# Three chunks of the last down product moved into the next turn, down products over three banks, and rows for outputs copied later

## The chip, the cores and the metric

One core of a Trainium2 chip runs the whole kernel. The metric is the device time of one execution in microseconds (us), lower is better. The engines are TensorE (PE for its matmuls, PEld for its weight loads), VectorE (DVE), ScalarE (ACT), GpSimd (POOL) and SyncE (SP), which issues the DMAs. Matmul results land in eight PSUM banks of 128 x 512 floats.

## The reference, cut to what matters

The kernel computes one decoder block on four sequences of 512 rows of 512 channels, in float32:

```
x = x + attention(layernorm(x))                    # 16 heads of 128
x = x + gamma * xattn(layernorm(x), ctx, ctx)      # 8 heads; a head is 64 rows of the sequence
h = layernorm(x)
x = x + (silu(h @ w1q.T) * (h @ w3q.T)) @ w2q.T    # 1365 hidden units, weights quantised to -s, 0, s
```

(The third layer norm is drawn in for the reader: the reference applies it to the argument of the feed-forward part.) The change touches the last two lines, computed for one sequence after another.

## The kernel before, in words

Stage A (to about 722 us) is the attention of all sequences. Stage B is the rest, and the change lies in it. Every product is done in two or three passes over a high and a low part of its operand, to keep float32's accuracy: so every tile has a part `...h` and a part `...l`, ScalarE writes the first, VectorE or GpSimd the second.

Stage B is a list of turns, `turns` (L411): (b, f) = (1, 0), (2, 1), (3, 2), (None, 3). A turn does the cross attention of sequence b beside the feed-forward part of sequence f, the one before it. All engines have their order written out by hand, in functions `pe_turn`, `act_turn`, `dve_turn`, `pool_turn` and `sp_rows`, and meet at semaphores. An engine does its instructions strictly in that order.

The first part of a turn has 32 steps n = 4h + q: head h of 8, query tile q of 4. In a step PE does one score tile (`pe_sx`, two matmuls of 512 columns into bank 0 or 1), the four transposes of a probability tile of the head before (`pe_pt`), in steps q = 1 and 3 half of a result (`pe_ret`, eight matmuls of 256 columns into bank 4), and one or no piece of the up product (`pe_up`). There are 22 pieces, for 11 chunks of hidden units (the last has 85) times the two weights w1 and w3; a piece is eight matmuls into bank 5 (w1) or bank 6 (w3). Piece 0, in step 1, comes in two halves of 256 columns, since the transposed rows `x3h` and `x3l` that it reads are only just made. ScalarE takes tanh, VectorE multiplies up (`dve_up`) and the gated hidden units lie in `gth` and `gtl`.

A score tile's bank is free again once VectorE has its row maximum (`dve_max`) and ScalarE its exponential (`act_exp`); with two banks, tile n + 2 waits for tile n. VectorE adds a head's result to the rows `x2` (`dve_ret`, two instructions, done for head h - 2 in steps with q = 2 from h = 2 on), and this also frees bank 4 (`r_free`) for the next head's `pe_ret`.

The end of a turn: `pe_down` for the four row tiles t = 0 to 3 of sequence f, each 11 chunks of two matmuls (22 of 512 columns) into `y_bank[t % 2]`, which is bank 7 or bank 5. Beside it VectorE makes the layer norm of sequence b (`dve_x3`, `dve_x3n`). PE then transposes tiles 0 and 1 of it (`pe_x3`), does the down product of t = 3, and transposes tiles 2 and 3; ScalarE writes `x3h` (`act_x3`), VectorE `x3l` (`dve_x3l`), which the next turn's piece 0 waits for. `dve_y` adds a down product to the rows `x2res`, and SP stores them to the output.

The rows `x2` are wanted twice: as the residual `x2res` of sequence f = b, and their place is filled with the next sequence's rows. In the first steps of the next turn GpSimd copies them tile by tile (`pool_keep`, L947, after all four output stores have landed), in steps 0 to 3. SP waits for the fourth copy and then loads the new 1 MB `x2` (L469), which `dve_ret` of head 0 waits for in step 10 (L787). In SP's order this load stands between the loads of head 2 and of head 3; each head has four loads of 128 KB (`sp_head`). They and this load go through one hardware queue.

Of the kernel before, what the change touches and what calls it, by code (L numbers as in the profile page):

```python
# [25 lines left out]
P = 128  # L26
B, T, C = 4, 512, 512
CK = C // P
TJ = T // P
# [6 lines left out]
XH, XD = 8, 64  # L36
SCALE_X = float(XD) ** -0.5
HID = int(2 * C * 4 / 3)
HC = -(-HID // P)
# [10 lines left out]
TANH_LAG, GATE_LAG = 1, 1  # L50
WARM = 34
RING_A = 4
WT = WS // 2
TERNARY = 3 * HID * C // WP // WT
SLOTS = 3 * CK + CK - 1
# [125 lines left out]
def decoder_block(nc, x, ctx, ctx_cols, wk, wq, wo, wvt, bk, bq, bv_col, bo, gamma, w1t, w3t, w2t, out):  # L181
# [7 lines left out]
    with stack:  # L189
# [129 lines left out]
        gth, gtl = put("gth", 136 * KB, [P, HC, T], F32R), put("gtl", 158 * KB, [P, HC, T], F32R)  # L319
        w2 = put("w2", 180 * KB, [P, HC, C], F32R)  # L320
        mem.close()
        u_bank, y_bank = bank[5:7], [bank[7], bank[5]]
        main = Mem(x1d=x1d, kd=kd, vd=vd, qst=qst, kh=kh, kl=kl, vts=vts, pe_x=pe_x, pxh=pxh, pxl=pxl, x2=x2,
                   s=bank[0:2], t=bank[2:4], r=bank[4], ring=2)

# [53 lines left out]
        def kept(f):  # L379
            return 16 + f * TJ  # L380
# [73 lines left out]
        def sp_rows(sp, b, f):  # L454

            if b is not None:
                sp.wait_ge(s[f"x1_out{b}"], 16)
                sp.wait_ge(s[f"st_out{b}"], 16)
                sp_stats(sp, b)
                sp_head(sp, main, b, 0)  # L460
                sp_head(sp, main, b, 1)
            if f is not None:
                for t in range(TJ):
                    sp.wait_ge(s["y"], 1 + f * TJ + (t + 1))
                    sp.dma_start(rows(out, f)[t * P:(t + 1) * P, :], x2res[:, t, :]).then_inc(s["y_out"], 16)
            if b is not None:
                sp_head(sp, main, b, 2)
                sp.wait_ge(s["x2_kept"], kept(b - 1))
                sp.dma_start(main.x2[:], rows(x1_dram, b).rearrange("(t p) c -> p t c", p=P)).then_inc(s["x2_in"], 16)  # L469
                for h in range(3, XH):  # L470
                    sp_head(sp, main, b, h)

        def sp_x2_back(sp):
# [95 lines left out]
        def pe_up(pe, f, piece):  # L569
            i, w = piece // 2, piece % 2  # L570
            m = chunk_rows(i)
            if piece == 0:
                pe.wait_ge(s["w_in"], 32)
                pe.wait_ge(s["out_free"], PASSES * GROUPS * PB * HG)
                pe.wait_ge(s["y"], 1 + f * TJ)
            pe.wait_ge(s[f"u{w}_free"], 1 + f * HC + i)

            for cols in (slice(0, T // 2), slice(T // 2, T)) if piece == 0 else (slice(0, T),):
                if piece == 0:
                    pe.wait_ge(s["t_free"], t_x3(f, cols.stop // P))  # L580
                for c in range(CK):
                    lhs = w13[:, w, c, i * P:i * P + m]
                    pe.matmul(u_bank[w][0:m, cols], lhs, x3h[:, c, cols], start=c == 0, stop=False)  # L583
                    mm = pe.matmul(u_bank[w][0:m, cols], lhs, x3l[:, c, cols], start=False, stop=c == CK - 1)  # L584
            mm.then_inc(s[f"u{w}_ready"], 1)

        def pe_down(pe, f, t, chunks=range(HC)):
            if 0 in chunks and t == 0:
                pe.wait_ge(s["w2_in"], 32)
            if 0 in chunks and t >= 2:  # L590
                pe.wait_ge(s["y"], 1 + f * TJ + (t - 1))
            if 0 in chunks and t == 1:
                pe.wait_ge(s["u0_free"], 1 + f * HC + HC)
            for i in chunks:
                k = chunk_rows(i)
                if t == 0:
                    pe.wait_ge(s["gl2"], 1 + f * HC + i + 1)
                pe.matmul(y_bank[t % 2][:], gth[0:k, i, t * P:(t + 1) * P], w2[0:k, i, :], start=i == 0, stop=False)  # L598
                mm = pe.matmul(y_bank[t % 2][:], gtl[0:k, i, t * P:(t + 1) * P], w2[0:k, i, :], start=False, stop=i == HC - 1)  # L599
            if HC - 1 in chunks:  # L600
                mm.then_inc(s["y_ready"], 1)

# [8 lines left out]
        def pe_turn(pe, b, f, nxt):  # L611
            for h in range(XH):
                for q in range(4):
                    if b is not None:
                        pe_sx(pe, main, b, h, q)
                        if h:
                            pe_pt(pe, main, b, h - 1, q)
                        if q == 1 and h >= 2:
                            pe_ret(pe, main, b, h - 2, 1)
                        if q == 3 and h >= 1:  # L620
                            pe_ret(pe, main, b, h - 1, 0)
                    if f is not None:
                        for piece in pieces(4 * h + q):
                            pe_up(pe, f, piece)
            if b is not None:
                pe_pt(pe, main, b, XH - 1, 0)
                pe_ret(pe, main, b, XH - 2, 1)
                pe_pt(pe, main, b, XH - 1, 1)
            if f is not None:
                pe_down(pe, f, 0, range(0, HC // 2))  # L630
            if b is not None:
                pe_pt(pe, main, b, XH - 1, 2)
            if f is not None:
                pe_down(pe, f, 0, range(HC // 2, HC))
            if b is not None:
                pe_pt(pe, main, b, XH - 1, 3)
                pe_ret(pe, main, b, XH - 1, 0)
            if f is not None:
                pe_down(pe, f, 1, range(0, 3))
            if b is not None:  # L640
                pe_ret(pe, main, b, XH - 1, 1)
            if f is not None:
                pe_down(pe, f, 1, range(3, HC))
                pe_down(pe, f, 2)
            if b is not None:
                pe_x3(pe, b, 0)
                pe_x3(pe, b, 1)
            if f is not None:
                pe_down(pe, f, TJ - 1)
            if b is not None:  # L650
                for t in range(2, TJ):
                    pe_x3(pe, b, t)
# [159 lines left out]
        def dve_y(dve, f, t):  # L812
            dve.wait_ge(s["y_ready"], f * TJ + (t + 1))
            if t == 0:
                dve.wait_ge(s["x2_kept"], kept(f))
            dve.scalar_tensor_tensor(x2res[:, t, :], y_bank[t % 2][:], wmean[:, 2:3], x2res[:, t, :],
                                     ALU.mult, ALU.add).then_inc(s["y"], 1)

        def dve_back(dve, link, k):
# [43 lines left out]
        def dve_turn(dve, b, f, nxt, between=None):  # L863
            for n in range(S_TILES):
                h, q = n // 4, n % 4
                if b is not None:
                    if q == 2 and h >= 2:
                        dve_ret(dve, main, b, h - 2)
                    dve_max(dve, main, b, h, q)
                if f is not None:  # L870
                    for piece in pieces(n - TANH_LAG):
                        dve_up(dve, f, piece)
                if b is not None:
                    if h:
                        dve_px(dve, main, b, h - 1, q)
                    if n:
                        dve_rinv(dve, main, b, (n - 1) // 4, (n - 1) % 4)
                    if prep_step(h) == n:
                        dve_q(dve, main, b, h + 1)
                    if q == 3 and h >= 4 and h % 2 == 0:  # L880
                        dve_moments(dve, main, b, (h - 4) // 2)
                    if between:
                        between(n)
# [25 lines left out]
            if b is not None:  # L909
                dve_x3l(dve, b, 0)  # L910
                dve_x3l(dve, b, 1)
            if f is not None:
                dve_y(dve, f, TJ - 1)
            if b is not None:
                for t in range(2, TJ):
# [43 lines left out]
        def pool_turn(pool, b, f, nxt):  # L959
            for n in range(S_TILES):  # L960
                h, q = n // 4, n % 4
                if b is not None:
                    if n:
                        pool_prob(pool, main, b, (n - 1) // 4, (n - 1) % 4)
                    if prep_step(h) == n - 1:
                        pool_prep(pool, main, b, h + 1)
                    if n - 1 in map(values_step, range(0, XH, 2)):
                        pool_vt(pool, main, b, (n - 1) // 8 * 2)
                if f is not None:
                    if f and n < TJ:  # L970
                        pool_keep(pool, f, n)
                    for piece in pieces(n - GATE_LAG):
                        pool_up(pool, f, piece)
            if b is not None:
                pool_prob(pool, main, b, XH - 1, 3)
            if f is not None:
                for n in range(S_TILES, S_TILES + GATE_LAG):
                    for piece in pieces(n - GATE_LAG):
                        pool_up(pool, f, piece)
            if nxt is not None:  # L980
                pool_prep(pool, main, nxt, 0)
                pool_prep(pool, main, nxt, 1)
# [1305 lines left out]
```

## Time and profile before

| | |
|---|---|
| time of three runs | 1113.26, 1113.51, 1113.57 us; median 1113.51 us |
| the profiled execution's own time | 1112.65 us |
| its span, first to last instruction | 1110.5 us |
| granted TensorE clock, mean | 1.00 of 2.4 GHz |
| PE busy | 1104.1 us, 99% of the span |
| DVE, ACT, POOL busy | 734.5, 550.0, 480.8 us |
| DMA | 122.20 MB, mean 110 GB/s |

Times within the profile are in us from the span's start. A matmul of 512 columns has a duration of 0.39 us in the rows, but the next one starts 0.23 us after it: they are pipelined, so what PE needs for a row of matmuls is read from start to start. For 256 columns the step is 0.12 us, for a transpose of 128 columns 0.10 us. A row may stand for several instructions (x2, x4, x8), and then has their duration together. In the square brackets stands how long the engine had been idle, and what released it.

### The profile page before, as it was taken

What the parts mean: (1) busy time and instruction counts of PE and PEld (TensorE: products, weight loads), DVE (VectorE), ACT (ScalarE), POOL (GpSimd) and SP (SyncE); (2) the same over time, 40 slices, a digit from 0 to 9 for tenths busy, and PEclk for the clock granted to TensorE, in tenths of its full rate; (3) what the DMA queues carried; (4) which work ended last, traced back from release to release, by engine and by line L of the source; (5) the groups of instructions that cost most, each with busy time, mean ns of one, the idle gap of its engine ahead of it and who ended that gap; (6) DMA issues with size and microseconds to landing.
All of it is one profiled execution on the core that took longest, in us unless ns stands there. A gap on an engine that the chain in (4) does not pass through costs nothing.

```text
span 1110.5 us, 15911 instructions
## 1 busy us (share of the span) xinstructions
PE 1104.1 (99%) x5840; PEld 939.0 (85%) x5840; DVE 734.5 (66%) x1347; ACT 550.0 (50%) x1149; POOL 480.8 (43%) x430
## 2 busy tenths in 40 slices
PE   9999999999999999999999999999999999999998
PEld 8888888888888888888888888888888888888886
DVE  7555547787877688866424344689967876887531
ACT  4556673325143376667605233177627763775130
POOL 1322345341324375665344040157628762875130
PEclk9999999999999999999999999999999999999999
DMA  7566553544533724212630221462213211410101
GB/s 247 164 190 189 184 178 124 177 126 152 182 109 94 229 96 143 86 39 86 253 114 2 75 86 39 139 205 66 54 50 100 76 49 58 114 48 2 38 1 38
DMA packets 54664, 122.20 MB, mean 110 GB/s; under 512 B 10058, under 2 KB 10058, under 8 KB 52539
## 3 DMA queue, kind: packets, MB, share of 16 engines
q1 hardware_dynamic: 54586, 121.18, 33.8%
q8 instruction: 47, 0.77, 0.3%
q14 instruction: 31, 0.25, 0.1%
HBM read 103.32 MB, written 17.84 MB: 109 GB/s over the span
## 4 chain that ended last, share of the span: by engine, by line
PE 97%; DVE 1%; ACT 1%; DMA 0%; issue 0%; POOL 0%; SPq 0%; POOLq 0%
PE bank L176 20%; PE bank L177 20%; PE bank L178 20%; PE bank L583 7%; PE bank L584 7%; PE bank L541 5%; PE bank L599 4%; PE bank L598 4%; PE bank L565 3%; PE bank L566 3%; PE bank L551 3%; PE bank L552 3%; PE bank L608 0%; DVE x3l L860 0%; PE bank L1278 0%; DMA xnf<-in_x 0%
## 5 line engine op out<-in xcount | busy, mean ns | idle before, releaser
L583 PE MATMUL bank<-x3h,w 128*128 128x512 f32 (+2 forms) x368 | 143.5, 393 | 0.4 <-DVE x3l L860 0.3
L584 PE MATMUL bank<-x3l,w 128*128 128x512 f32 (+2 forms) x368 | 140.6, 385 | 0.0
L1471 ACT ACTIVATE yh<-bank 128x512 fp32r<-128x512 f32 x64 | 38.1, 599 | 205.2 <-PE bank L178 205.2
L2152 POOL TENSOR_TENSOR wbl<-raw_b,wbh 128x512 fp32r<-128x512 f32 x64 | 85.7, 1358 | 58.6 <-ACT wbh L1534 58.2
L940 POOL TENSOR_SCALAR pe_x<-pe_x,xri,gam 128x512 f32<-128x512 f32 x96 | 75.5, 787 | 77.8 <-DVE xri L779 75.3
L775 DVE TENSOR_REDUCE xmx<-bank 128x1 f32<-128x512 f32 x128 | 87.7, 687 | 31.8 <-PE bank L552 30.5
L176 PE MATMUL bank<-wah,gh 128*128 128x512 f32 x256 | 102.6, 401 | 0.0
L176 PE MATMUL bank<-yh,rh 128*128 128x512 f32 x256 | 100.4, 392 | 0.1
L176 PE MATMUL bank<-wah,ph 128*128 128x512 f32 x256 | 100.1, 391 | 0.0
L177 PE MATMUL bank<-wal,gh 128*128 128x512 f32 x256 | 100.1, 391 | 0.0
L178 PE MATMUL bank<-wah,gl 128*128 128x512 f32 x256 | 100.0, 391 | 0.0
L178 PE MATMUL bank<-yh,rl 128*128 128x512 f32 x256 | 99.8, 390 | 0.0
L177 PE MATMUL bank<-wal,ph 128*128 128x512 f32 x256 | 99.7, 390 | 0.0
L178 PE MATMUL bank<-wah,pl 128*128 128x512 f32 x256 | 99.7, 389 | 0.0
L177 PE MATMUL bank<-yl,rh 128*128 128x512 f32 x256 | 99.7, 389 | 0.0
L2147 POOL TENSOR_TENSOR wal<-raw_a,wah 128x512 fp32r<-128x512 f32 x44 | 61.9, 1433 | 77.2 <-ACT wah L1513 77.2
L1803 DVE TENSOR_TENSOR yl<-bank,yh 128x512 fp32r<-128x512 f32 x64 | 44.0, 690 | 74.6 <-ACT yh L1471 74.6
L1983 DVE SCALAR_TENSOR_TENSOR xacc<-bank,rinv,xacc 128x512 f32<-128x512 f32 x64 | 47.9, 749 | 68.2 <-PE bank L178 66.7
L697 ACT ACTIVATE pe_x<-bank,xmx 128x512 f32<-128x512 f32 x96 | 66.0, 688 | 31.7 <-DVE xmx L775 31.3
L583 PEld LDWEIGHTS bank<-x3h,w 128*128 128x128 f32 (+1 forms) x368 | 68.2, 185 | 15.0 <-DVE x3l L860 0.7
L584 PEld LDWEIGHTS bank<-x3l,w 128*128 128x128 f32 (+1 forms) x368 | 68.2, 185 | 12.8
L1803 DVE TENSOR_TENSOR ml<-bank,mh 128x512 fp32r<-128x512 f32 x64 | 43.6, 686 | 53.0 <-ACT mh L1471 53.0
(181 smaller groups left out, 3016.6 us busy)
## 6 DMA issues: line engine op xcount, KB each, us to landing
raw_a<-in_wk SPq DMA_DIRECT2D x8, 1024.0 KB, 5.2
raw_b<-in_wq SPq DMA_DIRECT2D x8, 1024.0 KB, 6.7
raw_a<-in_wo SPq DMA_DIRECT2D x8, 1024.0 KB, 5.3
raw_b<-in_wvt SPq DMA_DIRECT2D x8, 1024.0 KB, 4.9
ternary_scratch<-wraw SPq DMA_DIRECT2D x24, 341.2 KB, 3.0
x1d<-x_scratch SPq DMA_DIRECT2D x48, 128.0 KB, 3.2
kd<-in_ctx SPq DMA_DIRECT2D x48, 128.0 KB, 3.2
w<-ternary_scratch SPq DMA_DIRECT2D x2, 2730.0 KB, 11.3
```

Source lines behind the costliest of these rows:

```text
L176: pe.matmul(out, wh, xh, start=start, stop=False, skip_group_check=shared)
L177: pe.matmul(out, wh, xl, start=False, stop=False, skip_group_check=shared)
L178: return pe.matmul(out, wl, xh, start=False, stop=stop, skip_group_check=shared)
L541: mm = pe.transpose(tb[:, c * P:(c + 1) * P], m.pe_x[:, q, c * P:(c + 1) * P], ident[:])
L583: pe.matmul(u_bank[w][0:m, cols], lhs, x3h[:, c, cols], start=c == 0, stop=False)
L584: mm = pe.matmul(u_bank[w][0:m, cols], lhs, x3l[:, c, cols], start=False, stop=c == CK - 1)
L697: act.activation(m.pe_x[:, q, :], m.s[q % 2][:], ACT.Exp, bias=xmx[:, q:q + 1], accum_out=xrs[:, q:q + 1]).then_inc(s["s_free"], 1)
L775: dve.reduce_max(xmx[:, q:q + 1], m.s[q % 2][:], axis=AX, negate=True).then_inc(s["xmx"], 1)
L940: pool.tensor_scalar(m.pe_x[:, q, :], m.pe_x[:, q, :], xri[:, q:q + 1], gam[:], ALU.mult, ALU.mult).then_inc(s["xpn"], 1)
L1803: dve.tensor_tensor(dst, a_bank(u)[:, cols], high.bitcast(F32), ALU.subtract).then_inc(s["a_free"], 1)
L2147: pool.tensor_tensor(wal[:, c, :], raw_a[:, c, :], wah[:, c, :].bitcast(F32), ALU.subtract).then_inc(s["wal_pool"], 1)
L2152: pool.tensor_tensor(wbl[:, c, :], raw_b[:, c, :], wbh[:, c, :].bitcast(F32), ALU.subtract).then_inc(s["wbl"], 1)
```

## The change

- Of the last down product (t = 3) of a sequence, PE does chunks 0 to 7 where it stood, and the last three (`DOWN_LATE`) in the next turn, after the score tile of step 1 and before piece 0. `dve_y` of this tile moves to step 1 of the next turn, after the row maximum of that step. The last turn has no next one and keeps its order.
- The four down products get banks 7, 5, 6 and 7. The waits follow: t = 2 waits for the last w3 piece to be read and no longer for the output of t = 0; t = 3 waits for the output of t = 0 only; pieces 0 and 1 wait for the outputs of t = 1 and t = 2 of the turn before, not for all four; t = 0 waits for the output of t = 3 of the turn before.
- GpSimd's copies `pool_keep` move from steps 0 to 3 to steps 3 to 6.
- SP's loads of head 3 move ahead of the wait for the copies and of the `x2` load behind it.

```diff
--- before.py
+++ after.py
@@ -50,6 +50,8 @@
 TANH_LAG, GATE_LAG = 1, 1
 WARM = 34
 RING_A = 4
+
+DOWN_LATE = 3
 WT = WS // 2
 TERNARY = 3 * HID * C // WP // WT
 SLOTS = 3 * CK + CK - 1
@@ -319,7 +321,7 @@
         gth, gtl = put("gth", 136 * KB, [P, HC, T], F32R), put("gtl", 158 * KB, [P, HC, T], F32R)
         w2 = put("w2", 180 * KB, [P, HC, C], F32R)
         mem.close()
-        u_bank, y_bank = bank[5:7], [bank[7], bank[5]]
+        u_bank, y_bank = bank[5:7], [bank[7], bank[5], bank[6], bank[7]]
         main = Mem(x1d=x1d, kd=kd, vd=vd, qst=qst, kh=kh, kl=kl, vts=vts, pe_x=pe_x, pxh=pxh, pxl=pxl, x2=x2,
                    s=bank[0:2], t=bank[2:4], r=bank[4], ring=2)
 
@@ -465,9 +467,10 @@
                     sp.dma_start(rows(out, f)[t * P:(t + 1) * P, :], x2res[:, t, :]).then_inc(s["y_out"], 16)
             if b is not None:
                 sp_head(sp, main, b, 2)
+                sp_head(sp, main, b, 3)
                 sp.wait_ge(s["x2_kept"], kept(b - 1))
                 sp.dma_start(main.x2[:], rows(x1_dram, b).rearrange("(t p) c -> p t c", p=P)).then_inc(s["x2_in"], 16)
-                for h in range(3, XH):
+                for h in range(4, XH):
                     sp_head(sp, main, b, h)
 
         def sp_x2_back(sp):
@@ -572,7 +575,9 @@
             if piece == 0:
                 pe.wait_ge(s["w_in"], 32)
                 pe.wait_ge(s["out_free"], PASSES * GROUPS * PB * HG)
-                pe.wait_ge(s["y"], 1 + f * TJ)
+            if piece < 2:
+
+                pe.wait_ge(s["y"], 1 + (f * TJ - 2 + piece if f else 0))
             pe.wait_ge(s[f"u{w}_free"], 1 + f * HC + i)
 
             for cols in (slice(0, T // 2), slice(T // 2, T)) if piece == 0 else (slice(0, T),):
@@ -587,16 +592,20 @@
         def pe_down(pe, f, t, chunks=range(HC)):
             if 0 in chunks and t == 0:
                 pe.wait_ge(s["w2_in"], 32)
-            if 0 in chunks and t >= 2:
-                pe.wait_ge(s["y"], 1 + f * TJ + (t - 1))
             if 0 in chunks and t == 1:
                 pe.wait_ge(s["u0_free"], 1 + f * HC + HC)
+            if 0 in chunks and t == 2:
+                pe.wait_ge(s["u1_free"], 1 + f * HC + HC)
+            if 0 in chunks and t == 0 and f:
+                pe.wait_ge(s["y"], 1 + f * TJ)
+            if 0 in chunks and t == TJ - 1:
+                pe.wait_ge(s["y"], 1 + f * TJ + 1)
             for i in chunks:
                 k = chunk_rows(i)
                 if t == 0:
                     pe.wait_ge(s["gl2"], 1 + f * HC + i + 1)
-                pe.matmul(y_bank[t % 2][:], gth[0:k, i, t * P:(t + 1) * P], w2[0:k, i, :], start=i == 0, stop=False)
-                mm = pe.matmul(y_bank[t % 2][:], gtl[0:k, i, t * P:(t + 1) * P], w2[0:k, i, :], start=False, stop=i == HC - 1)
+                pe.matmul(y_bank[t][:], gth[0:k, i, t * P:(t + 1) * P], w2[0:k, i, :], start=i == 0, stop=False)
+                mm = pe.matmul(y_bank[t][:], gtl[0:k, i, t * P:(t + 1) * P], w2[0:k, i, :], start=False, stop=i == HC - 1)
             if HC - 1 in chunks:
                 mm.then_inc(s["y_ready"], 1)
 
@@ -619,6 +628,8 @@
                             pe_ret(pe, main, b, h - 2, 1)
                         if q == 3 and h >= 1:
                             pe_ret(pe, main, b, h - 1, 0)
+                    if f and h == 0 and q == 1:
+                        pe_down(pe, f - 1, TJ - 1, range(HC - DOWN_LATE, HC))
                     if f is not None:
                         for piece in pieces(4 * h + q):
                             pe_up(pe, f, piece)
@@ -646,7 +657,7 @@
                 pe_x3(pe, b, 0)
                 pe_x3(pe, b, 1)
             if f is not None:
-                pe_down(pe, f, TJ - 1)
+                pe_down(pe, f, TJ - 1, range(HC if b is None else HC - DOWN_LATE))
             if b is not None:
                 for t in range(2, TJ):
                     pe_x3(pe, b, t)
@@ -813,7 +824,7 @@
             dve.wait_ge(s["y_ready"], f * TJ + (t + 1))
             if t == 0:
                 dve.wait_ge(s["x2_kept"], kept(f))
-            dve.scalar_tensor_tensor(x2res[:, t, :], y_bank[t % 2][:], wmean[:, 2:3], x2res[:, t, :],
+            dve.scalar_tensor_tensor(x2res[:, t, :], y_bank[t][:], wmean[:, 2:3], x2res[:, t, :],
                                      ALU.mult, ALU.add).then_inc(s["y"], 1)
 
         def dve_back(dve, link, k):
@@ -867,6 +878,8 @@
                     if q == 2 and h >= 2:
                         dve_ret(dve, main, b, h - 2)
                     dve_max(dve, main, b, h, q)
+                if f and n == 1:
+                    dve_y(dve, f - 1, TJ - 1)
                 if f is not None:
                     for piece in pieces(n - TANH_LAG):
                         dve_up(dve, f, piece)
@@ -909,7 +922,7 @@
             if b is not None:
                 dve_x3l(dve, b, 0)
                 dve_x3l(dve, b, 1)
-            if f is not None:
+            if f is not None and b is None:
                 dve_y(dve, f, TJ - 1)
             if b is not None:
                 for t in range(2, TJ):
@@ -967,8 +980,8 @@
                     if n - 1 in map(values_step, range(0, XH, 2)):
                         pool_vt(pool, main, b, (n - 1) // 8 * 2)
                 if f is not None:
-                    if f and n < TJ:
-                        pool_keep(pool, f, n)
+                    if f and 3 <= n < 3 + TJ:
+                        pool_keep(pool, f, n - 3)
                     for piece in pieces(n - GATE_LAG):
                         pool_up(pool, f, piece)
             if b is not None:
```

## Rows read from the trace of the kernel before

**Rows 1.** The page: shares of the chain that ended last, by engine.

```profile
PE 97%; DVE 1%; ACT 1%; DMA 0%; issue 0%; POOL 0%; SPq 0%; POOLq 0%
```

**Rows 2.** Stretches: PE, PEld, DVE, ACT, POOL busy; clock, DMA share, GB/s.

```profile
827.00:835.00 8.00, 7.86 (x47) 6.74 (x46) 4.09 (x7) 3.65 (x9) 1.94 (x3) 1.00 0.31 100
835.00:934.00 99.00, 99.00 (x562) 83.95 (x561) 80.73 (x167) 61.83 (x134) 64.89 (x64) 1.00 0.22 67
...
1042.00:1050.00 8.00, 7.62 (x44) 6.36 (x44) 2.73 (x4) 1.78 (x3) 2.21 (x4) 1.00 0.09 35
```

**Rows 3.** Timeline, PE alone, first to second sequence: start, duration, engine, line.

```profile
827.87 0.39 PE L598 MATMUL bank<-w,gth 128*128 128x512 f32 x1
...
829.25 1.04 PE L608 MATMUL bank<-ident,pe_x 128*128 128x128 f32 x8
830.04 0.48 PE L551 MATMUL bank<-kh,qst 128*128 128x512 f32 x1
...
832.85 0.28 PE L584 MATMUL bank<-x3l,w 128*128 128x256 f32 x1
833.27 0.50 PE L551 MATMUL bank<-kh,qst 128*128 128x512 f32 x1
```

**Rows 4.** Timeline, DVE and ACT, the same place.

```profile
831.72 1.28 DVE L775 TENSOR_REDUCE xmx<-bank 128x1 f32<-128x512 f32 x2
...
832.44 0.69 ACT L697 ACTIVATE pe_x<-bank,xmx 128x512 f32<-128x512 f32 x1 [1.46 <-DVE xmx L775]
```

**Rows 5.** Timeline, all engines, where the last turn begins.

```profile
1044.34 1.04 PE L608 MATMUL bank<-ident,pe_x 128*128 128x128 f32 x8
1044.54 0.75 DVE L816 SCALAR_TENSOR_TENSOR x2res<-bank,wmean,x2res 128x512 f32<-128x512 f32 x1 [3.55 <-PE bank L599]
...
1045.50 0.36 PE L583 MATMUL bank<-x3h,w 128*128 128x256 f32 x1
...
1045.61 1.29 DVE L860 TENSOR_TENSOR x3l<-bank,x3h 128x512 fp32r<-128x512 f32 x2 [0.32 <-ACT x3h L719]
...
1046.40 0.28 PE L584 MATMUL bank<-x3l,w 128*128 128x256 f32 x1
...
1046.95 0.39 PE L583 MATMUL bank<-x3h,w 128*128 128x256 f32 x1 [0.26 <-DVE x3l L860]
```

**Rows 6.** Timeline, POOL, early in the second sequence's turn.

```profile
839.27 0.61 POOL L950 COPY x2res<-x 128x512 f32<-128x512 f32 x1
...
842.23 0.77 POOL L940 TENSOR_SCALAR pe_x<-pe_x,xri,gam 128x512 f32<-128x512 f32 x1 [0.16 <-DVE xri L779]
...
844.40 1.30 POOL L934 TENSOR_TENSOR qst<-x1d,qst 64x512 fp32r<-64x512 f32 x1
845.94 0.77 POOL L940 TENSOR_SCALAR pe_x<-pe_x,xri,gam 128x512 f32<-128x512 f32 x1 [0.24 <-DVE xri L779]
```

**Rows 7.** Timeline, SP's DMA queue, the same turn.

```profile
832.45 1.06 SPq L436 DMA_DIRECT2D kd<-in_ctx  x1
...
839.91 0.38 SPq L469 DMA_DIRECT2D x<-x_scratch  x1
```

**Rows 8.** Timeline, ACT, the keys of head 2.

```profile
839.41 0.63 ACT L667 ACTIVATE kh<-kd 128x512 fp32r<-128x512 f32 x1
```

**Rows 9.** Landing of loads: all of x2, then kd from 825 to 850 us.

```profile
DMA to landing us min/median/max: 5.9/6.3/7.0
...
DMA to landing us min/median/max: 3.2/3.7/6.1
```

**Rows 10.** The page: a 1 MB load elsewhere; count, size, median us to landing.

```profile
raw_a<-in_wk SPq DMA_DIRECT2D x8, 1024.0 KB, 5.2
```

**Rows 11.** Timeline, DVE: the result of head 0 added to x2.

```profile
851.66 0.66 DVE L788 TENSOR_TENSOR x<-x,bank 64x512 f32<-64x512 f32 x1
852.36 0.69 DVE L790 TENSOR_TENSOR x<-x,bank 64x512 f32<-64x512 f32 x1
```

**Rows 12.** Timeline, PE: the next use of bank 4.

```profile
854.51 0.36 PE L565 MATMUL bank<-pxh,vts 128*128 128x256 f32 x1
```

## The prediction, made before the change was run

> **What bounds the kernel now.** The first view to read is the chain of what ended last: 97% of it is PE [rows 1]. The table of stretches says where PE is not busy in stage B: in the 99 us of a turn's middle it is busy for all 99.00, and in the 8 us around a change of sequence it loses 0.14 us by that count, around the start of the last turn 0.38 us [rows 2]. These counts are too kind, since a matmul's modelled end hides part of a gap, so the third view is the timeline of those places, read from start to start. The change takes no matmul away. It can only gain what PE loses at the three changes of sequence with a down product behind them (near 830, 938 and 1045 us), and it can lose whatever the moved copies and loads set off.
>
> **PE's work, moved.** Six matmuls (three chunks, two passes) leave the end of a turn. Before, the last six took from 827.87 to 829.25, which is 1.38 us [rows 3]. They come back after the second score tile, at the same step of 0.23 us. Net 0. What moves is everything between: the transposes of tiles 2 and 3 and both score tiles come 1.38 us earlier, piece 0 comes at the same time.
>
> **Gain at the second and third sequence.** The last half-width matmul of piece 0 starts at 832.85; the next could follow 0.12 us later, at 832.97, but the third score tile starts at 833.27. That is 0.30 us, and it has a duration of 0.50 instead of 0.39 us, since the pipeline was empty: 0.40 us in all [rows 3]. It waits for the first score bank: two row maxima from 831.72, the exponential from 832.44 to 833.13, having waited for the maximum [rows 4]. All of that hangs on the transposes and so comes 1.38 us earlier, the bank is free near 831.75, and PE asks at 832.97. The cover is 1.2 us. The displaced `dve_y` does not stand in this chain: it comes after both maxima, which end at 831.72 + 1.28 - 1.38 = 831.62, with its product ready at about 831.05 + 0.2; it runs to 832.37. Behind it the first reciprocal is late by about 0.4 us against what it could be, and GpSimd's scaling with it, but that is still 0.9 us earlier than before. The same pattern stands at 940.4 to 940.8. Gain 2 x 0.40 = 0.80 us.
>
> **Gain at the last turn.** No score tiles stand there. The eight transposes from 1044.34 take 0.79 us (829.25 to 830.04 in rows 3), but piece 0 begins at 1045.50 and not at 1045.13: it waits for the output of t = 3 to be added (1044.54 + 0.75 = 1045.29), 0.37 us. After its first half, at 1046.40 + 0.12, it waits for `x3l`, of which two tiles run from 1045.61 to 1046.90, until 1046.95: 0.43 us, and 0.11 us more duration [rows 5]. With the change piece 0 asks for the outputs of t = 1 only, added long before, and the six late matmuls cover the making of `x3l`, which then ends 1.38 us earlier, at 1045.52, before the second half asks at about 1046.1. Gain 0.91 us. Gains together 1.71 us; a smaller one, down to 0, only if something else is late there.
>
> **Banks and waits.** The t = 2 product gets a bank of its own. Its old wait for the output of t = 0, and that of t = 3 for t = 1, cost nothing: PE has no idle time there. Worth 0 on either side, by 0.1 us at most.
>
> **The copies and the load behind them: the price.** Before, GpSimd's fourth copy runs from 839.27 to 839.88 [rows 6], and SP issues the 1 MB load of `x2` at 839.91 [rows 7]. After, copies 2 and 3 (counted from 0) stand in steps 5 and 6, behind the preparation of head 2. GpSimd's scaling before that preparation, at 842.23, waited for VectorE [rows 6], so this part of GpSimd is paced by PE's steps, and shifts by the 0.40 us of the gain, not more. The last instruction of the preparation ends at 844.40 + 1.30 - 0.40 = 845.30. Then a copy (0.61), the scaling of step 5 (0.77, which no longer has to wait since it comes after the copy) and the last copy (0.61): 847.29, and the load goes out at 847.32, 7.4 us later than before [rows 6, 7]. It must land for VectorE's addition for head 0, at 851.66 before, 851.26 now; the two halves take until 853.05, 1.39 us [rows 11]; and PE needs them at 854.51 before, 854.11 now, to use bank 4 again [rows 12]. With a landing time L, and 0.1 us for the release, PE is ready at 847.32 + L + 1.49 = 848.81 + L. It waits L - 5.30 us, and 0.10 us for the refill. The slack before was 11.75 us for a load of 6; it is now 3.94 us on VectorE.
>
> L from the rows: the three loads of `x2` took 5.9, 6.3 and 7.0 us; the two at this place are the 5.9 and the 6.3 [rows 9]. A 1 MB load elsewhere takes 5.2 us in the median [rows 10]. The old place had the value load just ahead of it in the same queue; the new one has head 3's four loads well through and head 4's only behind. I take 5.7, between the ends 5.2 and 6.3. So 0.40 + 0.10 = 0.50 us at each of two turns, 1.0 us. The ends are 0 (L = 5.2) and 2 x 1.10 = 2.2 us (L = 6.3); at the very values before, 0.70 + 1.10 = 1.8 us. VectorE's other work after the delayed addition recovers: the next score bank is wanted at 857 us, some 2.5 us after its maximum can start.
>
> The Trainium skill ("DMA: Bandwidth & Descriptors", section "Anatomy of one DMA") gives a fit, for DMAs issued by GpSimd, of 2.0 us plus bytes over 436 GB/s. That would be 4.4 us for this load, an estimate by that page, and the wait would be gone. Every 1 MB load in the rows took longer.
>
> **Other loads.** SP's store of tile 3 goes out at about 832.40 instead of 830.23, and with it head 2's loads shift by 2.17 us: the last one, of keys, from 832.45 to 834.6 [rows 7]. Such loads take 3.2 to 3.7 us; the 6.1 is one behind the 1 MB load [rows 9]. It is there at 838.3, and ScalarE reads it at 839.41 - 0.40 = 839.01 [rows 8]. Cost 0, with 0.7 us to spare; with the cover gone a us of delay there would stand on ScalarE, which has slack against PE of under 1 us. The loads of head 3 come earlier than before and cost nothing. In the last turn the copies lie beside an idle GpSimd: 0.
>
> **Sum.** -1.71 + 1.0 = -0.7 us. Made against the profiled execution: 1112.65 us, of which 1110.5 is the span and 2.15 lies around it; it stands 0.86 below the median, so the difference is applied to the median: 1113.51 - 0.7 = 1112.8 us.
>
> **Rivals.**
> A, the load of `x2` is in time (L at most 5.3): all the gain is left, -1.7, 1111.8 us. For it: the 5.2 us row and an emptier queue. Against it: 5.9 and 6.3 at this very place.
> B, slower: the late load is the mechanism, VectorE stands at its addition for head 0 and PE behind it at bank 4. It decides from L = 6.06, where 2 x (L - 5.20) = 1.71. At 7.0, the longest of the three, 2 x 1.80 - 1.71 = +1.9, 1115.4 us. Or the issue is later than I make it by the same amount, since GpSimd's preparation is the long item there.
> C, the change doesn't do what it says: the third score tile or piece 0 waits for something else (the keys of head 2 late, the displaced addition in the way), and gain and price are both near 0: 1113.5 us.
>
> **How the numbers follow.** Forecast (L between 5.3 and 6.06) 0.52, A 0.22, B 0.18, C 0.08. 0.2%, 2.2 us, is about what a measurement of this kernel can tell from no change. Faster by that is above the whole gain of 1.71 and would need something that I don't see: 0.04. Slower by that needs L over 7.1 or a second wait: 0.07, out of B. The same: 0.89. The range takes in A with a little more, and B without its far end: 1111.6 to 1114.9 us.
>
> **What would show it.** In the new profile: no idle PE between piece 0 and the third score tile (832 to 834); piece 0 of the last turn in one run of sixteen half-width matmuls; the load of `x2` issued near 847.3; VectorE idle before the first addition of a head's result, put down to a DMA, 1 to 2 us, and PE idle near 854 before the first result product of head 1, by 0.3 to 1.0 us, in both turns. I am wrong if PE is idle elsewhere, if the copies end before the preparation of head 2, or if the difference is beyond 2 us.

## The result: 1114.96 us, slower by 0.17%

The changed kernel takes 1114.96 us in the median of 22 runs (1113.93 to 1117.68), the kernel before 1113.36 us on the same chips. The ratio is 1.0017, with a 95% interval of 1.0011 to 1.0023: slower by 1.9 us, 1.2 to 2.6. The forecast was 1112.8 us in a range up to 1114.9. The sign was wrong, and what came true is the mechanism of rival B: the load of `x2` is late, and the wait for it costs more than the gain. The profiled execution has a span of 1112.9 us against 1110.5.

First the page's shares of the chain that ended last, of the changed kernel. Where there was 97% PE and no DMA [rows 1], DMA now has 2% (1% is the load of `x2`, by the page's next line):

```profile
PE 95%; DMA 2%; DVE 1%; POOL 1%; ACT 1%; issue 1%; SPq 0%; POOLq 0%; DVEq 0%
```

The stretches (PE, PEld, DVE, ACT, POOL busy, then clock, DMA share, GB/s) answer to [rows 2]. The changes of sequence are gap-free, and the middles of the turns have lost 1.15 and 1.75 us:

```profile
827.00:835.00 8.00, 8.00 (x48) 7.00 (x47) 4.38 (x8) 4.18 (x9) 0.77 (x1) 1.00 0.15 52
835.00:934.00 99.00, 97.85 (x555) 82.52 (x554) 80.15 (x166) 61.69 (x134) 66.12 (x66) 1.00 0.24 69
...
943.00:1042.00 99.00, 97.25 (x550) 81.93 (x549) 78.40 (x164) 59.02 (x128) 61.05 (x62) 1.00 0.19 54
```

PE's order at the first change of sequence (start, duration, engine, line), to read beside [rows 3]: the late chunks end, piece 0 follows, and the third score tile comes 0.13 us after its last matmul, with a duration of 0.40 and not 0.50 us:

```profile
828.09 1.04 PE L617 MATMUL bank<-ident,pe_x 128*128 128x128 f32 x8
...
831.05 0.39 PE L608 MATMUL bank<-w,gtl 85*128 85x512 f32 x1
831.27 0.28 PE L588 MATMUL bank<-x3h,w 128*128 128x256 f32 x1
...
833.04 0.29 PE L589 MATMUL bank<-x3l,w 128*128 128x256 f32 x1
833.17 0.40 PE L554 MATMUL bank<-kh,qst 128*128 128x512 f32 x1
```

GpSimd after it answers to [rows 6]. The third and fourth copies (L963) stand behind the preparation of head 2, which ends at 844.91 + 1.30. The second row, the scaling ahead of that preparation, waited 0.88 us for VectorE, where it had waited 0.16:

```profile
839.08 1.29 POOL L970 TENSOR_TENSOR gtl<-gf,gth 128x512 fp32r<-128x512 f32 x1
...
842.73 0.77 POOL L953 TENSOR_SCALAR pe_x<-pe_x,xri,gam 128x512 f32<-128x512 f32 x1 [0.88 <-DVE xri L790]
...
844.91 1.30 POOL L947 TENSOR_TENSOR qst<-x1d,qst 64x512 fp32r<-64x512 f32 x1
846.27 0.61 POOL L963 COPY x2res<-x 128x512 f32<-128x512 f32 x1
...
847.58 0.61 POOL L963 COPY x2res<-x 128x512 f32<-128x512 f32 x1
```

So SP issues the load at 848.22 (before 839.91, [rows 7]); the two loads at this place land after 6.1 and 6.7 us (5.9 and 6.3 in [rows 9]):

```profile
848.22 0.38 SPq L472 DMA_DIRECT2D x<-x_scratch  x1
```

The line that groups these loads, and the landing of all three loads of `x2` (the 5.5 is the first, which stands elsewhere):

```profile
L472 SPq DMA_DIRECT2D x<-x_scratch x2: 382/382/383, 848.2 to 957.0; - x2
...
DMA to landing us min/median/max: 5.5/6.1/6.7
```

VectorE waits for it (to be read beside [rows 11]). Its first line here, the scaling of head 2's rows `x1d`, is another matter, taken up below:

```profile
839.37 1.29 DVE L775 TENSOR_SCALAR x1d<-x1d,stx 128x512 f32<-128x512 f32 x1
...
854.41 0.68 DVE L799 TENSOR_TENSOR x<-x,bank 64x512 f32<-64x512 f32 x1 [2.57 <-DMA x<-x_scratch]
855.12 0.69 DVE L801 TENSOR_TENSOR x<-x,bank 64x512 f32<-64x512 f32 x1
```

And PE waits for VectorE, at the place of [rows 12]. The first line is the last half-width matmul ahead of head 2's first score tile (eight up matmuls stand between), the second that tile, the third the transposes before the wait, the last the next use of bank 4:

```profile
844.08 0.28 PE L569 MATMUL bank<-pxl,vts 128*128 128x256 f32 x1
...
846.26 0.50 PE L554 MATMUL bank<-kh,qst 128*128 128x512 f32 x1
...
854.24 0.60 PE L544 MATMUL bank<-ident,pe_x 128*128 128x128 f32 x4
855.96 0.36 PE L568 MATMUL bank<-pxh,vts 128*128 128x256 f32 x1 [1.12 <-DVE x L801]
```

**The account by turns.** The transposes of tiles 0 and 1 (eight at once, behind the third down product) are a good mark, since nothing around them changed. In the kernel before and in the changed one:

```profile
823.34 1.04 PE L608 MATMUL bank<-ident,pe_x 128*128 128x128 f32 x8
...
930.89 1.04 PE L608 MATMUL bank<-ident,pe_x 128*128 128x128 f32 x8
...
1038.44 1.04 PE L608 MATMUL bank<-ident,pe_x 128*128 128x128 f32 x8
```

```profile
823.56 1.04 PE L617 MATMUL bank<-ident,pe_x 128*128 128x128 f32 x8
...
932.33 1.04 PE L617 MATMUL bank<-ident,pe_x 128*128 128x128 f32 x8
...
1041.70 1.04 PE L617 MATMUL bank<-ident,pe_x 128*128 128x128 f32 x8
```

The turn of the second sequence went from 107.55 to 108.77 us, that of the third from 107.55 to 109.37. From the last mark to the start of the last matmul of all it was 68.47 us and is 67.54. Together +1.22 + 1.82 - 0.93 = +2.11 us. In the second turn the wait at bank 4 is 855.96 - 854.24 - 0.36 = 1.36 us (the transposes alone take 0.36; the 1.12 in brackets counts from their modelled end). At the first score tile of head 2 PE loses another 0.3 us: it starts 2.18 us after the last half-width matmul (844.08 to 846.26), where it was 1.98, and its first matmul then needs 0.34 us from start to start and not 0.23. It follows the end of head 2's preparation, 844.91 + 1.30 = 846.21. So 1.66 us are lost and 0.44 gained. In the third turn, by the same reading of its rows, it is 1.96 + 0.30 lost and 0.44 gained.

### The profile page after: what moved, and what is told of

Its sections match the earlier page's. It is cut to its first block, busy times and chain, and to the rows that moved or that the text cites. A ratio compares the mean times of both kernels' runs of the same rounds, so it can differ in the third digit from the quotient of the medians.

```text
span 1112.9 us, 15915 instructions
## 1 busy us (share of the span) xinstructions
PE 1103.1 (99%) x5840; PEld 937.8 (84%) x5840; DVE 733.8 (66%) x1347; ACT 550.8 (49%) x1149; POOL 481.0 (43%) x430
## 4 chain that ended last, share of the span: by engine, by line
PE 95%; DMA 2%; DVE 1%; POOL 1%; ACT 1%; issue 1%; SPq 0%; POOLq 0%; DVEq 0%
PE bank L178 20%; PE bank L179 20%; PE bank L180 20%; PE bank L588 6%; PE bank L589 6%; PE bank L544 4%; PE bank L608 4%; PE bank L607 4%; PE bank L568 3%; PE bank L569 3%; PE bank L554 2%; PE bank L555 2%; DMA x<-x_scratch 1%; PE bank L617 1%; DMA xnf<-in_x 0%
```

## The experiments

All kernels ran beside the kernel before on the same chip. Where a time differs by less than 1 us the turn lengths of the profile say more than the medians: the first of these marks lies between 823.3 and 827.5 us in the profiled executions, though most of what comes before it is the same in all kernels. The kernel before had 1113.79 us beside the first four of them and 1113.37 beside the other four. "Turn 2" and "turn 3" are from mark to mark as above, "end" is from the third mark to the start of the last matmul.

| kernel | median us | ratio to before, interval | turn 2 | turn 3 | end |
|---|---|---|---|---|---|
| before | 1113.36 | | 107.55 | 107.55 | 68.47 |
| changed | 1114.96 | 1.0017 (1.0011 to 1.0023) | 108.77 | 109.37 | 67.54 |
| keep1 | 1112.48 | 0.9985 (0.9976 to 0.9993) | 107.59 | 107.48 | 67.59 |
| late_copies | 1117.09 | 1.0023 (1.0013 to 1.0032) | 109.34 | 109.33 | 68.47 |
| banks | 1113.36 | 0.9993 (0.9985 to 1.0002) | 107.54 | 107.54 | 68.42 |
| keep5 | 1126.59 | 1.0112 (1.0095 to 1.0129) | 115.08 | 113.77 | 67.58 |
| keep1233 | 1111.84 | 0.9985 (0.9976 to 0.9994) | 107.11 | 107.11 | 67.54 |
| split | 1112.03 | 0.9986 (0.9977 to 0.9995) | 107.36 | 107.42 | 67.56 |
| hold | 1119.09 | 1.0050 (1.0036 to 1.0064) | 110.20 | 111.64 | 67.60 |
| keep1_late1 | 1112.58 | 0.9994 (0.9985 to 1.0003) | 107.50 | 107.50 | 68.06 |

**The copies earlier (keep1).**

```diff
-                    if f and 3 <= n < 3 + TJ:
-                        pool_keep(pool, f, n - 3)
+                    if f and 1 <= n < 1 + TJ:
+                        pool_keep(pool, f, n - 1)
```

> The changed kernel with GpSimd's four copies in steps 1 to 4 instead of 3 to 6, nothing else. Theory (the late load): in the changed kernel the load of x2 is issued 8.3 us later than before and lands 2.6 and 3.2 us after VectorE asks; PE loses 1.36 and 1.96 us at bank 4 for it. Copies 0 to 3 in steps 1 to 4 end before head 2's preparation, the load goes out near 842 us, lands near 848 and nobody waits: PE's gap before the first result product of head 1 is gone in both turns, and the time falls by 3.3 us or a little more, to about 1111.5 us, 1.8 under the kernel before. Rival (late chunks or banks themselves cost): the time stays above the kernel before. Rival (collision of GpSimd and VectorE at the preparation of head 2): the gap at bank 4 goes, but PE's wait of 0.3 us before the first score tile of head 2 stays and so does VectorE's 1.28 us for the scaling of head 2's rows.

The time fell under that of both kernels: the ratio 0.9985 is 1.7 us under the kernel before, where 1.8 was expected. No wait at bank 4 is left in turns 2 and 3. But they take 107.59 and 107.48 us and not 107.15: the 0.3 us before head 2's first score tile stayed, with VectorE's long `x1d`, as the collision rival had it. The late load is the main loss; there is a second, small thing beside it.

**The late copies alone (late_copies).** The kernel before with

```diff
-                    if f and n < TJ:
-                        pool_keep(pool, f, n)
+                    if f and 3 <= n < 3 + TJ:
+                        pool_keep(pool, f, n - 3)
...
                 sp_head(sp, main, b, 2)
+                sp_head(sp, main, b, 3)
                 sp.wait_ge(s["x2_kept"], kept(b - 1))
...
-                for h in range(3, XH):
+                for h in range(4, XH):
```

> The kernel before with only the copies moved to steps 3 to 6 and head 3's loads ahead of the x2 load; three chunks and banks as before. Theory (the late load): this part alone is the loss. The same two gaps at bank 4 appear, 1.4 to 2.0 us each, with 0.3 us each before head 2's first score tile, and without the gain of 1.7 us the time is 3.7 us above before, 1117 us (1116 to 1118). Rival (late chunks or banks cost): less than 1.5 us above before.

Turns 2 and 3 are longer by 1.79 and 1.78 us with no late chunk in the kernel, and the end is as before. That is 3.6 us, the 3.7 of the expectation; the medians say 3.3 and the ratio 2.6 us (1.4 to 3.6). PE's wait at bank 4 in its turn 2:

```profile
857.52 0.35 PE L566 MATMUL bank<-pxh,vts 128*128 128x256 f32 x1 [1.29 <-DVE x L791]
```

**Banks and waits alone (banks).** The changed kernel without the late chunks, with the old place of the last `dve_y`, of the copies and of head 3's loads.

> The changed kernel with only its banks and waits: the three chunks, the last output, copies and loads stand where they stood before. Theory: no effect, within 0.2 us; the timeline of a change of sequence is that of before. In the last turn piece 0 starts 0.37 us earlier, at once behind the transposes, but its second half still waits for x3l at the same moment, so that is not a gain. Rival (banks are worth something by themselves): over 0.5 us either way.

Turns of 107.54, end 68.42: nothing. In the last turn piece 0 starts at once behind the transposes from 1044.94, where it started 1.16 us behind them [rows 5], and its second half then waits so much longer for `x3l`:

```profile
1044.94 1.04 PE L616 MATMUL bank<-ident,pe_x 128*128 128x128 f32 x8
1045.73 0.36 PE L587 MATMUL bank<-x3h,w 128*128 128x256 f32 x1
...
1047.55 0.39 PE L587 MATMUL bank<-x3h,w 128*128 128x256 f32 x1 [0.63 <-DVE x3l L868]
```

**More of the cause (keep5).** Copies in steps 5 to 8.

> The changed kernel with the copies two steps later still, in steps 5 to 8: more of the suspected cause. Theory (the late load): the load goes out about 2.6 us later again, and PE's gap at bank 4 grows by as much, to 4 and 4.6 us: 5.2 us above the changed kernel, 1120 us (1119 to 1122), the last score tiles behind it perhaps late as well. The preparation of head 2 no longer has copies ahead of it: its 0.3 us may go. Rival (the load is not what counts): the time stays near 1115 us.

The sign and the place are as expected, the size is twice as large: turns longer by 6.3 and 4.4 us than in the changed kernel, the time by 11.6. The load went out 23.6 us behind the transposes of tiles 2 and 3, 3.5 later than in the changed kernel and not 2.6, so PE stood for 5.1 us. And behind that wait PE's clock was at the lower level of 1.2 GHz for some 6 us: the granted clock (the third number from the end) reads 0.50, and the half-width matmuls come every 0.21 us, not 0.12. So this turn is 8.0 us longer than keep1233's 107.11. The stretches around the wait, and PE's first rows after it:

```profile
856.00:861.00 5.00, 0.03 (x1) 0.06 (x1) 1.52 (x3) 0.00 (x0) 1.78 (x2) 0.91 0.86 246
861.00:864.00 3.00, 3.00 (x11) 2.80 (x12) 2.32 (x5) 2.42 (x6) 0.77 (x1) 0.50 0.00 0
864.00:867.00 3.00, 3.00 (x8) 2.20 (x7) 0.84 (x3) 0.61 (x2) 1.95 (x2) 0.51 0.00 0
```

```profile
860.97 0.55 PE L568 MATMUL bank<-pxh,vts 128*128 128x256 f32 x1 [5.08 <-DVE x L801]
...
861.53 0.41 PE L568 MATMUL bank<-pxh,vts 128*128 128x256 f32 x1
```

The third turn of this kernel had a wait of 4.93 us, and the clock behind it was low for a shorter time:

```profile
976.00:979.00 3.00, 3.00 (x12) 2.71 (x13) 2.31 (x5) 2.50 (x6) 0.77 (x1) 0.53 0.00 0
979.00:982.00 3.00, 3.00 (x16) 2.41 (x16) 1.78 (x5) 1.11 (x4) 2.02 (x2) 0.90 0.00 0
```

Of the 6.3 us in turn 2, 4.0 are the longer wait (5.08 against 1.12) and most of the rest is the lower clock, which my expectation had not counted. Its guess about head 2 came true: `x1d` starts late within `gtl` and takes 0.72 us, and the first score tile of head 2 does not wait.

```profile
840.73 0.72 DVE L775 TENSOR_SCALAR x1d<-x1d,stx 128x512 f32<-128x512 f32 x1
...
844.25 1.29 POOL L943 TENSOR_TENSOR kl<-kd,kh 128x512 fp32r<-128x512 f32 x1
```

**The collision (keep1233).** Copies in steps 1, 2, 3 and 3.

```diff
-                    if f and 3 <= n < 3 + TJ:
-                        pool_keep(pool, f, n - 3)
+                    if f:
+                        for t in {1: (0,), 2: (1,), 3: (2, 3)}.get(n, ()):
+                            pool_keep(pool, f, t)
```

> The changed kernel with GpSimd's copies in steps 1, 2, 3 and 3, so that two copies and not one stand ahead of the making of gtl in step 3. Base: with the copies in steps 1 to 4 a turn took 107.59 and 107.48 us between the transposes of tiles 0 and 1 (before: 107.55 both), and there VectorE's scaling of head 2's rows (x1d) took 1.47 us, not 0.6, having started 0.1 us after GpSimd's gtl. Theory (collision): x1d is held while GpSimd's two-input instruction runs; with a second copy ahead, gtl starts 0.5 us after x1d, x1d takes 0.6 us again, PE's wait of 0.3 us before head 2's first score tile goes, a turn takes 107.15 us, and the time is 0.5 to 0.7 us under that of copies in steps 1 to 4, about 1111.8. Rival (the wait is from GpSimd's own queue, not from the collision): x1d is short but PE still waits before head 2's first score tile, the turn stays at 107.5.

As the theory had it, to a few hundredths: turns of 107.11 us. In keep1 `x1d` started 0.11 us after GpSimd's `gtl` and took 1.47 us. With a second copy ahead of `gtl`, it starts in the copies and takes 0.76. The rival, GpSimd's own queue, is out: in keep1 the scaling ahead of head 2's preparation had stood idle 0.87 us for VectorE. In keep1, VectorE, then GpSimd:

```profile
843.33 1.47 DVE L775 TENSOR_SCALAR x1d<-x1d,stx 128x512 f32<-128x512 f32 x1
...
843.22 1.30 POOL L970 TENSOR_TENSOR gtl<-gf,gth 128x512 fp32r<-128x512 f32 x1
...
846.87 0.77 POOL L953 TENSOR_SCALAR pe_x<-pe_x,xri,gam 128x512 f32<-128x512 f32 x1 [0.87 <-DVE xri L790]
847.60 1.30 POOL L943 TENSOR_TENSOR kl<-kd,kh 128x512 fp32r<-128x512 f32 x1
```

In keep1233:

```profile
840.10 0.76 DVE L775 TENSOR_SCALAR x1d<-x1d,stx 128x512 f32<-128x512 f32 x1
...
839.41 1.17 POOL L963 COPY x2res<-x 128x512 f32<-128x512 f32 x2
840.54 1.47 POOL L970 TENSOR_TENSOR gtl<-gf,gth 128x512 fp32r<-128x512 f32 x1
...
843.66 1.30 POOL L943 TENSOR_TENSOR kl<-kd,kh 128x512 fp32r<-128x512 f32 x1
```

The preparation of head 2 starts 15.55 us behind the transposes of tiles 2 and 3 in keep1 (832.05 to 847.60) and 14.84 us in keep1233 (828.82 to 843.66). PE's wait before head 2 is gone, and this is the fastest kernel of the study, 1111.84 us, though the interval of its time does not part it from keep1 and split; the turns do.

**The first tile of the load early, the copies late (split).**

```diff
+                sp.wait_ge(s["x2_kept"], kept(b - 1) - (TJ - 1))
+                sp.dma_start(main.x2[:, 0], rows(x1_dram, b)[0:P]).then_inc(s["x2_in_first"], 16)
                 sp.wait_ge(s["x2_kept"], kept(b - 1))
-                sp.dma_start(main.x2[:], rows(x1_dram, b).rearrange("(t p) c -> p t c", p=P)).then_inc(s["x2_in"], 16)
+                sp.dma_start(main.x2[:, 1:TJ], rows(x1_dram, b)[P:T].rearrange("(t p) c -> p t c", p=P)).then_inc(s["x2_in"], 16)
```

`dve_ret` waits for `x2_in_first` with head 0 and for `x2_in` with head 2.

> The changed kernel, copies in steps 3 to 6 as it has them, but the load of x2 in two: tile 0, which the first addition needs, right behind the first copy, the other three tiles behind the fourth. Theory (the late load): the copies' place on GpSimd is harmless by itself; tile 0 lands near 842 us, the rest is wanted only by head 2 of 8; no wait at bank 4. PE's 0.3 us before head 2's first score tile stay. A turn 107.45 us, time 1.8 us under before with 0.3 us each taken off: about 1112.3. Rival (copies among GpSimd's scaling work delay the probabilities): PE is idle elsewhere in steps 5 to 12 and the turns are over 108 us.

Turns of 107.36 and 107.42, time 1112.03. The copies' own place costs nothing beyond the 0.3 us of the collision, which is in this kernel too (107.11 + 0.3). What the first addition needs went out at 841.39 and landed 3.1 us later, after the 842 of the expectation but in good time. The rest went out at 849.28 and harmed nobody.

**The load held back, the copies early (hold).** keep1, and ahead of SP's load `sp.wait_ge(s["xpn"], b * S_TILES + 7)`.

> The changed kernel with copies in steps 1 to 4, but SP holds the load of x2 back until GpSimd has scaled the probability tile of step 6: the load goes out about 21.2 us after the transposes of tiles 2 and 3, against 20.1 in the changed kernel and 14.0 with copies in steps 1 to 4. Theory (the late load): the gap at bank 4 is back though no copy is late, 1 us larger than in the changed kernel: 2.4 and 3.0 us, turns of 110.0 to 110.5 us, time about 1117 (1116 to 1118). Rival (the copies' place costs, not the load): the time stays at 1112.5.

This is the counterpart of split: early copies and a late load give the gap back. It is 2.46 us in turn 2, which is as expected, and 2.3 us in turn 3, where 3.0 was expected and the turn is nevertheless longer than turn 2 by 1.4 us: behind that wait, and not behind the other, the granted clock was low for a part. So the time, 1119.09 us, lies above the expected 1116 to 1118. PE after the wait, and two stretches behind it:

```profile
967.79 0.36 PE L569 MATMUL bank<-pxh,vts 128*128 128x256 f32 x1 [2.30 <-DVE x L802]
```

```profile
967.70:970.00 2.30, 2.21 (x11) 2.04 (x12) 1.93 (x4) 1.60 (x4) 0.75 (x1) 0.68 0.00 0
970.00:973.00 3.00, 3.00 (x12) 2.38 (x11) 1.48 (x4) 1.43 (x4) 1.15 (x3) 0.68 0.00 0
```

**One chunk instead of three (keep1_late1).** keep1 with `DOWN_LATE = 1`.

> Copies in steps 1 to 4, but one chunk moved into the next turn instead of three (two matmuls, 0.46 us). Theory (the gain is cover for two waits of 0.30 us behind the transposes, and of 0.43 us for x3l in the last turn): 0.46 us covers all of them, just. At the changes of sequence the third score tile still follows piece 0 at once, and the two halves of piece 0 in the last turn run together. Time equal to that with three chunks within 0.3 us, about 1112.5. Rival (three chunks are needed, since the chain behind the transposes has more in it than its visible waits): gaps of 0.1 to 0.3 us are left in each place.

Half right. At the changes of sequence one chunk is enough: turns of 107.50 us, like keep1. In the last turn it is not: the end takes 68.06 us, of the 0.93 us gain 0.41 is there. The second half of piece 0 still waits:

```profile
1045.57 1.04 PE L617 MATMUL bank<-ident,pe_x 128*128 128x128 f32 x8
...
1047.75 0.28 PE L589 MATMUL bank<-x3l,w 128*128 128x256 f32 x1
1048.18 0.39 PE L588 MATMUL bank<-x3h,w 128*128 128x256 f32 x1 [0.15 <-DVE x3l L871]
...
1046.84 1.29 DVE L871 TENSOR_TENSOR x3l<-bank,x3h 128x512 fp32r<-128x512 f32 x2 [4.16 <-ACT x3h L730]
```

The expectation took the wait for `x3l` as 0.43 us, as [rows 5] show it. But `x3l` is ready some 2.6 us after the transposes begin (1045.57 to 1048.18 here, 1044.34 to 1046.95 there), and PE gets to the second half 1.75 us after them if nothing else holds it. The earlier wait of 0.37 us had hidden a part of this one. So the cover needed is 0.86 us. By that estimate two chunks (0.92 us) are enough, which was not run, and three have 0.5 us to spare.

## Why the prediction was wrong, point by point

- **The gains were right.** Forecast 0.40 + 0.40 + 0.91 = 1.71 us; measured 0.44 + 0.44 + 0.93 = 1.81 us (keep1233, which has nothing else in it: 107.55 - 107.11, twice, and 68.47 - 67.54).
- **Banks and waits** at nothing: right, shown by `banks`.
- **Other loads** at nothing: right as far as it went; no wait of ScalarE for head 2's keys in the changed kernel.
- **The copies and the load behind them** is the step that failed, by the size of its terms and by one term that it left at nothing. The mechanism was as written: copies behind head 2's preparation, load late, VectorE at head 0's addition, PE at bank 4. The forecast had 1.0 us for both turns; PE waited 1.36 + 1.96 = 3.32. Two terms of the sum were too small. The landing time: I took 5.7 us, between this place's 5.9 and 6.3 and a 5.2 from elsewhere, on the argument that nothing would be ahead of it; measured were 6.1 and 6.7, 1.4 us in all, with head 4's four loads right behind (last section). The issue: forecast 847.32; measured 848.22, of which 0.22 us is a later start of the whole turn, so 0.68 us late per turn, 1.36 in all. Of these 2.76 us PE felt 2.3, since it came to bank 4 later itself, by about the 0.3 us of the next point.
- **A term was missing.** I shifted GpSimd's preparation of head 2 with PE, on the ground that the scaling ahead of it waited for VectorE. It did, but VectorE was late itself. With one copy fewer ahead of it, `gtl` starts at 839.08, before `x1d` at 839.37, and `x1d` takes 1.29 instead of 0.60 us; the score maximum, the probability tile and the preparation all follow it. This cost 0.3 us in each turn at head 2's first score tile; keep1 and keep1233 show it from both sides. It also made most of the load's delay. The 0.68 us are all there at the start of head 2's preparation: it starts 19.91 us behind the first mark in the changed kernel (843.47 - 823.56), where the forecast has 842.97 - 0.40 - 823.34 = 19.23. In the two kernels with a short `x1d` it starts after 19.34 us (keep5, 844.25 - 824.91) and 19.37 us (keep1233, 843.66 - 824.29). So some 0.55 us of the 0.68 go with the collision; the last 0.1 us no run explains.
- **Rival B** had the right mechanism, and the point from which it decides, L = 6.06, was right for my issue time. For the changed kernel as it ran I estimate 5.35: its two landings are 6.4 us in the mean, and each us of landing costs two, one in each turn, so the loss of 2.11 us is gone at 1.05 us less. Every whole load of `x2` in this study took longer, 5.5 us at least, so by this estimate the change could not win at any landing time seen, with its copies where it has them. It had 0.18; the values of this very place, 5.9 and 6.3, already put the sum at +0.1, and they deserved more weight than a load from another stage.
- **Rival A** (load in time) needed L of 5.3 at most; no load of `x2` as a whole took under 5.5. The Trainium skill ("DMA: Bandwidth & Descriptors", "Anatomy of one DMA") gives, by its fit for GpSimd-issued DMAs, an estimate of 4.4 us for this size. These loads are issued by SP and took 5.5 to 6.7 us at this place, and the measurement decides.
- **What would show it:** all signs named in the forecast were there in kind, but three were too large: the load was issued 0.9 us later than named, VectorE stood idle for a DMA before the addition for 2.6 us and not 1 to 2, and PE near bank 4 for 1.4 and 2.0 us and not 0.3 to 1.0. One that it said would prove it wrong was there too: PE idle elsewhere, at head 2's first score tile.

## What to carry to other kernels

A copy that frees a buffer is the head of a chain: moved by a few steps, it moves the load behind it, and the load's full landing time then counts from there. Add up copy, landing and first reader against the slack before moving it, with the longest landing seen at that place and not a mean with others; even that, 6.3 us here, was short of the 6.7 that came. And when work is taken from the front of a busy in-order engine, look at what its next instructions will now run beside.

## What the runs showed of the hardware

- **VectorE and GpSimd hold each other up for some pairs of instructions.** VectorE's `x1d` (one float32 input and output in SBUF) takes 0.53 us alone. Where it began within an instruction of GpSimd, it ended 0.27 to 0.29 us behind the end of that one, however early it had begun: it took 1.47 us when it began 0.11 us into `gtl` (keep1), 1.29 when 0.29 us into it (changed kernel), 0.72 when 0.86 us into it (keep5). A copy of GpSimd did the same (1.00 us in keep1_late1, 0.59 in the kernel before). Where `x1d` was first, `gtl` took 1.47 us and not 1.29 (keep1233). This agrees with the Trainium skill ("SBUF — State Buffer", "Who interferes with whom"), by which a VectorE `tensor_scalar` can enter a mode that takes the ports shared with GpSimd, and the later of the two is then fully blocked; that the mode was on, the trace does not show. The cost here was not the 0.7 us but the chain behind it.
- **TensorE's clock can fall behind a wait of a few microseconds.** Behind 5.1 and 4.93 us of idle PE (keep5) it was at or near 1.2 GHz for about 6 and 3 us; behind 2.3 us (hold, turn 3) the mean was 0.68 over 5 us; behind 2.46 us (hold, turn 2) it stayed at 1.00. What makes the difference between the last two, no run here shows.
- **Neighbours in the queue seem to slow a 1 MB load, behind it as well as ahead.** Where the next load was issued 3.5 us or more behind it and the last one 2.4 us ahead (keep1, keep1_late1), `x2` landed after 5.5, 5.5, 5.5 and 5.8 us. With head loads right behind it and none for 8 us ahead (changed kernel, late_copies, keep5, hold) it took 6.1 to 6.7. With head loads right behind and the value load 1.9 us ahead (before, banks) it took 5.9 to 6.3, and with head loads right ahead only (keep1233) 5.7 and 6.4. The spread within a pair is up to 0.7 us, as large as the difference, so this is an observation and no more.
